# A graph layer with nearest-neighbour scores on one core: POOL scales and splits the rows x of each group of the score stage, and takes two instead of four subtractions of the last stage

## The reference

```python
# x: 8192 x 128, A: 8192 x 8192 (sparse values, stored dense), W1, W2: 128 x 128
def lap(A, x):
    d = 1.0 / sqrt(sum(A, axis=-1))
    return d[:, None] * (A @ (d[:, None] * x))
z   = leaky_relu(lap(A, x) @ W1 + b1, 0.1)
d2  = maximum(sq[:, None] + sq[None, :] - 2 * (z @ z.T), 0)     # sq = sum(z*z)
S   = exp(-sqrt(d2 + 1e-10) / 2)
S   = where(rank of S in its row < 4, S, 0)                     # the 4 nearest rows
out = layernorm(x + lap(S + A, x) @ W2 + b2)
```

## Time and profile before

| what | us |
|---|---|
| median of three executions | 2832.22 |
| the profiled execution | 2839.99 |
| its span, first to last instruction | 2838.1 |
| PE busy | 2545.1 |
| DVE busy | 2408.6 |
| ACT busy | 1582.5 |
| POOL busy | 980.0 |

### The profile page before, as it was taken

One profiled execution on the slowest core, in us unless ns is written; L12 is line 12 of the kernel. 1 busy time (PEld: TensorE's weight loads), 2 busy tenths in 40 slices (PEclk: granted clock), 3 DMA queues, 4 the chain that ended last, 5 costly groups with the idle time before them and its releaser, 6 DMA issues.

```text
span 2838.1 us, 28440 instructions
## 1 busy us (share of the span) xinstructions
PE 2545.1 (90%) x9592; PEld 1780.5 (63%) x9592; DVE 2408.6 (85%) x1667; ACT 1582.5 (56%) x1806; POOL 980.0 (35%) x708
## 2 busy tenths in 40 slices
PE   1477999999899998889999999999999997998898
PEld 0133444444577776568778787878778775466665
DVE  7988898876788887999999999998999977288887
ACT  0000000001377767679989898988989884266764
POOL 0000000000000000016566565656666675667770
PEclk9688999999999999999999999999999998999999
DMA  9999999995788850014455554554454669999996
GB/s 385 422 398 377 386 421 421 421 403 204 293 317 332 333 198 30 0 60 141 141 153 143 150 151 143 144 155 140 131 158 141 174 179 408 378 362 327 356 351 227
DMA packets 144632, 713.43 MB, mean 251 GB/s; under 512 B 18624, under 2 KB 26560, under 8 KB 82560
## 3 DMA queue, kind: packets, MB, share of 16 engines
q1 hardware_dynamic: 123072, 669.71, 62.9%
q0 software_dynamic: 16832, 33.84, 5.0%
q10 hardware_dynamic: 4608, 8.39, 0.8%
HBM read 679.62 MB, written 32.24 MB: 251 GB/s over the span
## 4 chain that ended last, share of the span: by engine, by line
PE 56%; DVE 19%; DMA 10%; ACT 7%; issue 5%; POOL 2%; SPq 1%; DVEq 0%; ACTq 0%
PE PS L571 14%; DVE R L1216 6%; PE PS L661 5%; PE PS L662 5%; PE PS L663 5%; DVE R L1222 5%; DMA cache<-at 5%; DMA ring<-at 4%; PE PS L749 3%; PE PS L703 3%; PE PS L694 3%; PE PS L695 3%; DVE al_t L1295 3%; PE PS L631 3%; PE PS L665 3%
## 5 line engine op out<-in xcount | busy, mean ns | idle before, releaser
L1025 POOL TENSOR_TENSOR al<-ring,ah 128x1024 fp32r<-128x1024 f32 x252 | 605.8, 2410 | 432.3 <-ACT ah L878 432.2
L1216 DVE MAX8 R<-R 128x8 f32<-128x8192 f32 x64 | 556.2, 8691 | 91.9 <-ACT R L910 89.5
L910 ACT ACTIVATE R<-PS 128x1024 f32<-128x1024 f32 x512 | 523.0, 1022 | 183.9 <-PE PS L663 107.8
L1222 DVE FIND_INDEX8 R<-R,R 128x8 uint32<-128x8192 f32 x64 | 555.9, 8685 | 0.0
L661 PE MATMUL PS<-zh,zst 128*128 128x512 f32 x1024 | 413.9, 404 | 64.5 <-ACT PS L895 57.0
L1010 POOL CAST zst<-zh 128x128 fp32r<-128x128 f32 (+1 forms) x64 | 28.0, 438 | 1217.2 <-DVE zl L1168 878.6
L662 PE MATMUL PS<-zl,zst 128*128 128x512 f32 x1024 | 404.0, 395 | 0.0
L663 PE MATMUL PS<-zh,zst 128*128 128x512 f32 x1024 | 403.9, 394 | 0.0
L571 PE MATMUL PS<-cache,R 128*128 128x512 f32 x680 | 309.7, 611 | 29.9 <-DVE R L1114 15.9
L1071 POOL DMA_INDIRECT R<-xs_dram,R x256 | 269.5, 1053 | 118.2 <-issue 81.1
L661 PEld LDWEIGHTS PS<-zh,zst 128*128 128x128 f32 x1024 | 195.3, 191 | 133.8 <-ACT PS L895 71.5
(11 more groups left out here) (149 smaller groups left out, 4174.0 us busy)
## 6 DMA issues: line engine op xcount, KB each, us to landing
R<-at SPq DMA_DIRECT2D x151, 1024.0 KB, 7.9
ring<-at SPq DMA_DIRECT2D x144, 1024.0 KB, 6.9
ring<-at SPq DMA_DIRECT2D x252, 512.0 KB, 3.9
cache<-at SPq DMA_DIRECT2D x125, 1024.0 KB, 18.3
raw_sq<-at SPq DMA_DIRECT2D x22, 1024.0 KB, 7.5
raw_z<-at SPq DMA_DIRECT2D x21, 1024.0 KB, 7.7
raw_ring<-at SPq DMA_DIRECT2D x21, 1024.0 KB
acc_dram<-R POOLq DMA_DIRECT2D x63, 256.0 KB, 5.7
```

Source lines behind the costliest of these rows:

```text
L910: act.activation(score[j % 2][:, c * EC:(c + 1) * EC], PS[:, 2 * (c % 2):2 * (c % 2) + 2].rearrange("p b c -> p (b c)"), ACT.Copy).then_in ...
L1025: pool.tensor_tensor(al[:, k % SPLIT], raw[k % RAW], ah[:, k % SPLIT].bitcast(F32), ALU.subtract)\
L1216: v.max(top[:, j], score[j % 2]).then_inc(dve3, 1)
L1222: v.max_index(place[:, j], top[:, j], score[j % 2]).then_inc(placed, 1)
```

## The change

POOL makes the three operations of `scale_xg`. They stand in its program at cells (2, 0), (2, 1) and (2, 2), each with its waits: for DVE's scales (new semaphore `d2_ok`), for the pieces and stores that still read the old halves, and between the operations themselves. DVE raises `d2_ok` instead, and waits in `scale_of_rows` until the group before is through (`xg_ok`). `GAP` goes from 2 to 4, so that a group's first piece stands in cell (2, 5). Group 7's x has no halves and is still scaled by DVE. `BY_POOL` goes from 4 to 2; with it ACT's distances and roots of group 7 move, ACT's to quads 2 and 3, DVE's to 3 and 4.

```diff
-BY_POOL = 4
+BY_POOL = 2
...
-        CHA, CHN, CHB = 2, 2, 9
+        CHA, CHN, CHB = 2, 2, 8
...
-        LATE, GAP, NP = 2, 2, HB * PIECES
+        LATE, GAP, NP = 2, 4, HB * PIECES
...
+                if u == BY_POOL:
+                    s_of_distances(G - 1)
                 if u == BY_POOL + 1:
-                    s_of_distances(G - 1)
-                if u == BY_POOL + 2:
                     root_of_sums(G - 1)
...
+            def scale_xg(g):
+                pool.wait_ge(s_xn, 16 * (g + 1))
+                hold(pool)
+                pool.wait_ge(d2_ok, g + 1)
+                hold(pool)
+                pool.tensor_tensor(xg, xg, bcast(tiny[:, 4], D), ALU.mult).then_inc(xg_scaled, 1)
+
+            def high_of_xg(g):
+                if not is_first(g):
+                    pool.wait_ge(prodb, NP * g)
+                    hold(pool)
+                    pool.wait_ge(s_split, 32 * g)
+                    hold(pool)
+                pool.wait_ge(xg_scaled, g + 1)
+                hold(pool)
+                pool.tensor_copy(xgh[:, :, :], xg).then_inc(xgh_ok, 1)
+
+            def low_of_xg(g):
+                pool.wait_ge(xgh_ok, g + 1)
+                pool.tensor_tensor(xgl[:, :, :], xg, xgh[:, :, :].bitcast(F32), ALU.subtract).then_inc(xg_ok, 1)
+
...
                     for c in range(NE):
+                        if not first and (j, c) == (2, 0):
+                            scale_xg(g - 1)
+                        if not first and (j, c) == (2, 1):
+                            high_of_xg(g - 1)
+                        if not first and (j, c) == (2, 2):
+                            low_of_xg(g - 1)
...
                 scale_of_rows(g, lk)
-                scale_xg(g, lk)
+                v.sem_inc(d2_ok, 1)
...
                 v.wait_ge(root2_ok, g + 1)
+                if not is_first(g):
+                    hold(v)
+                    v.wait_ge(xg_ok, g)
                 newton(lk, tiny[:, 0], tiny[:, 1], tiny[:, 3], tiny[:, 2], d2g)
...
-                lk(v.tensor_tensor(xg, xg, bcast(d2g, D), ALU.mult))
-                if not is_first(g):
-                    v.wait_ge(prodb, NP * g)
-                    hold(v)
-                    v.wait_ge(s_split, 32 * g)
-                v.tensor_copy(xgh[:, :, :], xg).then_inc(xgh_ok, 1)
-                v.wait_ge(xgh_ok, g + 1)
-                v.tensor_tensor(xgl[:, :, :], xg, xgh[:, :, :].bitcast(F32), ALU.subtract).then_inc(xg_ok, 1)
```

More of the change, by code:

```diff
@@ L342, in build @@
         xgh_ok = sem("xgh_ok")
+        d2_ok = sem("d2_ok")
+        xg_scaled = sem("xg_scaled")
         rnd_t = sem("rnd_t")
@@ L1258, in scale_of_rows, with scale_last_xg @@
                 lk(v.tensor_copy(d2s[:, tiles], d2g))
-            def scale_xg(g, lk):
-                d2g = tiny[:, 4]
+            def scale_last_xg(g):
                 v.wait_ge(s_xn, 16 * (g + 1))
-                if isinstance(g, int) and g == G - 1:
-                    v.tensor_tensor(xg, xg, bcast(d2g, D), ALU.mult).then_inc(xg_ok, 1)
-                    return
-                lk(v.tensor_tensor(xg, xg, bcast(d2g, D), ALU.mult))
-                if not is_first(g):
-                    v.wait_ge(prodb, NP * g)
-                    hold(v)
-                    v.wait_ge(s_split, 32 * g)
-                v.tensor_copy(xgh[:, :, :], xg).then_inc(xgh_ok, 1)
-                v.wait_ge(xgh_ok, g + 1)
-                v.tensor_tensor(xgl[:, :, :], xg, xgh[:, :, :].bitcast(F32), ALU.subtract).then_inc(xg_ok, 1)
+                v.tensor_tensor(xg, xg, bcast(tiny[:, 4], D), ALU.mult).then_inc(xg_ok, 1)
             def group_dve(g):
@@ L1357, in _ @@
                     scale_of_rows(G - 1, lk)
-                    scale_xg(G - 1, lk)
+                    scale_last_xg(G - 1)
                 if not plain[u]:
```

## The result

| | us |
|---|---|
| changed kernel, median of 4 | 2803.72 (2802.65 to 2804.43) |
| kernel before, median of 4 beside it | 2833.71 (2832.13 to 2835.3) |
| ratio | 0.9889, 95% interval 0.9878 to 0.9901 |
| forecast | 2797, range 2787 to 2814 |

What follows compares the result with a forecast made beforehand. DVE's work at each group's start, then PE, was taken as the bound. Gains of 31.5 (groups 2 to 6), 2.0 and 2.3 less 1.1 made 34.7 us, from the median 2832.22 to 2797 us, range 2787 to 2814.

Steps and rivals of the forecast that it cites:

- The bound of a group: Score stage, group start: DVE delays ACT's copy and PE's seed; PE's 4.64 us wait becomes about 0.5, group 153.6 us.
- The clock: PE behind cell (3, 1): 12 matmuls at the lower clock cost 2.45 us more; this goes with the wait.
- rival B: Score stage: the wait goes but a clock fall stays in every group, costing 12.3 us, total 2810; chance 8%.
- POOL's handover: Group start: POOL's three operations end 6.7 us after POOL is free; PE waits 0.2 us at cell (2, 5), at most 1.7.
- The gain of a group: Steady groups 2 to 6: 7.1 us gained less 0.8 charged for PE's remaining waits, 6.3 us each, 31.5 in all.
- A: Cell (2, 5): POOL hands over late, PE waits 2 to 3 us and the clock falls; total 2821; chance 12%.
- D: Group start: one POOL operation is held for a whole DVE scan, 8.69 us; slower, total 2867; chance 4%.
- F: Tile 1: POOL's subtraction holds FIND_INDEX8 up to 2.4 us; 10.5 us less gain, total 2808; chance 3%.
- G: Group start: DVE's new wait for `xg_ok` holds it as long as the operations did; total 2832; chance 2%.
- Groups 1 and 7: Score stage, first and last changed groups: gains of 2.0 us in group 1 and 2.3 in group 7.
- The last stage: After the scores: earlier gathers take bandwidth, 1.1 us lost; bounds 8 us gained and 4 lost.
- Rival C: Last stage: later quads follow the earlier roots and subtractions, 8 us more gained, total 2789; chance 11%.

## Why the prediction was right, and where it was off

**The bound of a group** held. The wait of ACT for FIND_INDEX8 fell from 4.8 to 1.2 us, and groups 2 to 6 take 153.6 to 153.7 us where 153.6 was forecast. That DVE's time there is worth its length, and in most groups the clock's fall behind it, is shown from both sides, by the change and by the DVE operation put in again (3.4 us gave 4.8 us a group in the mean).

**The clock** was at its full level once the wait was gone, so rival B fell. But the length of a wait alone does not tell whether the fall comes. The forecast put only 1.41 us on the side without it; 2.83 us in the earlier trace rows had no slow matmuls behind it either, nor had 2.27 us in two groups with the old gap and 3.50 us in one group of the run with the longer DVE, while 2.08 and 3.30 us had them. What else decides is not shown.

**POOL's handover** was sized too high, on the safe side: the multiplication took 1.90 us (forecast 2.40), the cast 1.04 (1.4), the subtraction 2.40, in all 5.6 with the steps instead of 6.7. I had PE waiting 0.2 us; POOL was 1.66 us early. Of this difference of 1.9 us, 1.1 are POOL's shorter operations, 0.2 its being free sooner, and the other 0.5 a short wait of PE for ACT at cell (2, 4). The sum had left that wait out, since in the kernel before a piece stood ahead of that cell and PE did not wait there:

```profile
1408.92 0.50 PE L663 MATMUL PS<-zh,zst 128*128 128x512 f32 x1 [0.37 <-ACT PS L897]
```

**The gain of a group** came out right with two terms that cancel. In group 2, from which it was sized, it is 159.91 - 153.61 = 6.3 us, the forecast. Of the 7.1 us 6.9 are there (4.58 of the wait and 2.31 of the slow matmuls: the 12 behind it now take 2.86 us). The 0.8 us charged for POOL and the rest of the wait are not, but 0.5 goes to the new wait at cell (2, 4). The mean of 6.6 comes of groups 3 to 6, which took 160.1 to 160.4 us in the kernel before and not group 2's 159.9.

**Rivals.** A's mechanism is real: it is the run with the old gap, where PE waits for POOL and the clock falls in most groups. It did not strike because of the two cells. D fell: POOL's operations at 1405 to 1410.6 were not drawn out beside DVE's MAX8 (L1049 took 2.40 us). F did not show, though its case, POOL's subtraction beside a FIND_INDEX8, did not arise for tile 1: MAX8 lasted until 1411.2. The 64 FIND_INDEX8 of the changed kernel took 8683 to 8690 ns, 56 of them beside a POOL operation with two inputs. G fell with the table.

**Groups 1 and 7** came within 0.2 us of the forecast, with some luck in the terms. In group 1 the work alone gave 2.9 us (forecast 3.4; the run with the old gap has 152.7) and the pieces' move took 1.1 (1.4). In group 7 the work alone cost 1.8 us (170.1) and the move alone 2.2 (170.5), and only together they gain 2.2; the forecast's reason, DVE's waits at tiles 2 and 3, was not tested.

**The last stage** is the term that was mis-sized: a loss of 1.1 us was forecast and 4.9 measured, 0.9 beyond the bound of 4, which the prediction itself names as a sign of being wrong. The step that failed is "Gathers beside it take bandwidth: 391 GB/s with them against 423 without, 7%". The direction was right, as the run with later gathers shows, but the row was misread. In the kernel before, from 2390 to 2395, all packets, then those of the loads' queue:

```profile
DMA packets 835, 1.96 MB, mean 391 GB/s; under 512 B 16, under 2 KB 16, under 8 KB 791
...
q1 hardware_dynamic: 834, 1.94, 100.6%
```

No gather moved in that window; the first was issued at 2391.2, and its packets came later. The lower rate goes with the small packets, most likely those of the light blocks' sums, whose load SP issued at 2385.4: the run without gathers has 398 GB/s at 2350 to 2360, with 1174 of 1376 packets under 8 KB. And a total rate has the gathers' own bytes in it. The loads alone lost 18%, as shown above. The gathers now stand beside the loads for 28.6 us ahead of the 14th quad and not for 11.5; 18% of the 17.1 us more is 3.1 us (an estimate), and the quad did come 3.1 us later. The second part was left out altogether: PE, idle for 6.6 us, took up its work at the lower clock (0.63 us a matmul) and lost another 1.8 us up to the first plain quad (7.3 us from the rounding to it, before 5.5). I had priced that in the score stage and not here. Rival C (8 us gained) fell: with the earlier roots and the gathers held back the last stage takes 481.2 us, as with the old roots.

**The median.** Of the 6.7 us between 2797 and 2803.7, 3.8 are the last stage, -1.0 the groups, 1.5 the median of before, which was 2832.2 when I forecast and 2833.7 beside the result, and 0.5 the rounding of 2797.5. The remaining 1.9 us were not traced; they are within what the stages ahead of group 0's end vary by.

## What to carry to other kernels

When the work of one engine is moved off a chain, ask for the first cell in which the result is wanted and put the consumer a cell or two behind it: here the two cells' shift was worth 16.8 of 36.8 us, and by itself it cost 6.8. A wait of the matrix engine has to be priced with the slower matmuls that may follow, 1.6 to 2.6 us behind waits of 2.1 to 4.6 us here and none behind a few of 2.3 to 3.5 us, at each place in the program. And a result that comes sooner may start transfers sooner: here, in a stretch with a full DMA share, they took time from the loads that end last, and holding them until those were in took the loss back. What they take is read from the bytes of each queue, not from the total rate.

## What the runs showed of the hardware that was not expected

POOL multiplied 128x1024 by a broadcast operand in 1.90 us, where its subtraction of two full operands takes 2.40; on DVE both took 1.23. The two also differ in the type that they write, so what makes POOL's multiplication shorter is not shown. POOL's cast of 128x1024 took 1.04 us, 2.3 times less than the subtraction. The gathers, some 50 of the 386 GB/s in 20 us of full queues, went with loads that moved 18% less. And in two sets of runs the last stage took some 60 to 100 us more for every kernel, at a DMA share of mostly 0.6 to 0.9 instead of 0.9 to 1.0, with the score stage unchanged to 0.5 us.
